# Softmax attention: each step weighs its values in two halves of 256 queries

## What is computed

```python
B, L, D = x.shape                      # 8, 512, 128
H, hd = 16, 8
q = apply_rope((x @ Wq.T + bq).reshape(B, L, H, hd))
k = apply_rope((x @ Wk.T + bk).reshape(B, L, H, hd))
v = (x @ Wv.T + bv).reshape(B, L, H, hd)
scores = einsum('bqhd,bkhd->bhqk', q, k) / sqrt(hd)
attn = softmax(scores, axis=-1)
out = einsum('bhqk,bkhd->bqhd', attn, v).reshape(B, L, D)
x = x + out @ Wo.T + bo
```

## Time and profile before

| | |
|---|---|
| median of 3 runs | 1422.12 us (1420.34 to 1422.55) |
| span of the profiled execution (first to last instruction) | 1422.4 us |
| the attention's exponentials | 267 to 699 us of the span |
| TensorE busy | 1176.4 us (83%) |
| VectorE busy | 825.7 us (58%) |
| ScalarE busy | 721.3 us (51%) |
| mean granted TensorE clock | 0.929; full between 284 and 711 us |

### The profile page before, as it was taken

How to read it: one execution, slowest core, us unless ns; L and a number is a source line. 1 busy time by engine, 2 the same in 40 slices (tenths; PEclk the granted TensorE clock), 3 DMA queues, 4 the chain that set the end, 5 groups by cost and what they waited for, 6 DMA issues and landing times.

```text
span 1422.4 us, 23037 instructions
## 1 busy us (share of the span) xinstructions
PE 1176.4 (83%) x7234; PEld 782.2 (55%) x7234; DVE 825.7 (58%) x2697; ACT 721.3 (51%) x1451; POOL 721.7 (51%) x949
## 2 busy tenths in 40 slices
PE   4289997899999999999789998329999777389994
PEld 3278986122233232232278987218799556268894
DVE  7611265898898999998442666702216687421235
ACT  4244443477767767677544555213445575234441
POOL 3776754202424435523764477744554277625543
PEclk9999999699999999999979999659999898589997
DMA  9577887535435343341357886425577031145586
GB/s 292 149 198 213 243 234 243 163 102 167 133 103 174 103 118 118 88 136 49 117 140 222 258 234 185 146 78 167 161 211 245 28 132 36 49 133 177 175 260 199
DMA packets 166377, 226.82 MB, mean 159 GB/s; under 512 B 22960, under 2 KB 125744, under 8 KB 166256
## 3 DMA queue, kind: packets, MB, share of 16 engines
q1 hardware_dynamic: 121456, 174.04, 42.3%
q0 software_dynamic: 18304, 37.65, 7.7%
q10 hardware_dynamic: 26496, 13.64, 3.3%
HBM read 152.81 MB, written 72.20 MB: 158 GB/s over the span
## 4 chain that ended last, share of the span: by engine, by line
PE 54%; DVE 14%; POOL 10%; DMA 8%; issue 6%; ACT 5%; SPq 3%; ACTq 0%; POOLq 0%; DVEq 0%
PE PS L1416 17%; PE PS L1406 16%; POOL dispatched L736 8%; DVE arena L2300 5%; PE PS L1584 5%; PE PS L1560 5%; DMA arena<-experts 3%; ACT arena L1131 2%; PE PS L1396 2%; PE PS L1568 2%; PE PS L1546 2%; DMA YC<-expert_out 1%; DVE BST L1858 1%; DVE X L1868 1%; DMA expert_out<-arena 1%
## 5 line engine op out<-in xcount | busy, mean ns | idle before, releaser
L1004 ACT ACTIVATE arena<-PS,arena 128x256 f32<-128x256 f32 (+1 forms) x568 | 267.4, 498 | 367.7 <-PE PS L1406 355.8
L764 POOL DMA_INDIRECT expert_out<-arena x316 | 304.5, 964 | 281.7 <-issue 192.9
L1131 ACT ACTIVATE arena<-PS 128x512 f32<-128x512 f32 x512 | 283.9, 596 | 134.8 <-PE PS L1560 133.9
L2300 DVE TENSOR_REDUCE arena<-PS 128x2 f32<-128x1024 f32 x256 | 300.9, 1217 | 28.8 <-PE PS L1570 27.9
L1406 PE MATMUL PS<-arena 128*128 128x256 f32 (+1 forms) x1136 | 309.0, 415 | 9.8 <-DMA arena<-experts 7.5
L1416 PEld LDWEIGHTS PS<-arena 128*128 128x128 f32 x2528 | 303.9, 192 | 18.7 <-issue 4.0
L1416 PE MATMUL PS<-arena 128*128 128x128 f32 x2528 | 306.7, 275 | 3.2 <-DVE arena L2123 3.2
L2123 DVE TENSOR_TENSOR arena<-PS,arena 128x256 f32<-128x256 f32 (+1 forms) x142 | 64.5, 454 | 369.5 <-PE PS L1416 369.5
L1406 PEld LDWEIGHTS PS<-arena 128*128 128x128 f32 x1136 | 210.0, 195 | 59.8 <-DMA arena<-experts 10.1
L736 POOL DMA_INDIRECT dispatched<-arena x192 | 185.3, 965 | 81.7 <-issue 57.9
L1560 PE MATMUL PS<-arena 96*128 96x512 bf16 x512 | 174.2, 391 | 10.5 <-ACT arena L1131 4.7
(11 more groups left out here) (274 smaller groups left out, 1177.3 us busy)
## 6 DMA issues: line engine op xcount, KB each, us to landing
arena<-experts SPq DMA_DIRECT2D x142, 578.0 KB
qk_products<-arena SPq DMA_DIRECT2D x48, 384.0 KB, 4.4
arena<-qk_products SPq DMA_DIRECT2D x64, 288.0 KB
arena<-dispatched SPq DMA_DIRECT2D x110, 129.0 KB, 3.0
dispatched<-FILL SPq DMA_DIRECT2D x32, 322.5 KB, 2.8
YC<-expert_out ACTq DMA_DIRECT2D x40, 256.0 KB
arena<-qk_products SPq DMA_DIRECT2D x64, 128.0 KB, 5.1
arena<-dispatched SPq DMA_DIRECT2D x32, 193.5 KB, 4.0
```

What stands on the lines that cost most here:

```text
L764: pool.indirect_dma_start(YK, bass.IndirectOffsetOnAxis(ap=ID[:, s:s + 1], axis=0), YS[:, s, :], None).then_inc(s_yo[r], 16)
L1004: act.activation(HT[:, tau % PAIR, q, 0:S * P], hidden_chunk(S, q), func, bias=WE[:, r, 2 * DFF + q:2 * DFF + q + 1]).then_inc(s_g, 1)
L1131: act.activation(PT[:, G % 2, j, k, :], bank(4 + k % 2), ACT.Exp, scale=float(1.0 / np.sqrt(HD))).then_inc(s_exp, 1)
L2300: dve.tensor_reduce(MX[:, G % 2, head:4:2, a], PS[:, 1024 * w:1024 * w + 1024].rearrange("p (a b) -> p a b", a=2), AX_X, ALU.max).then_inc ...
```

## The change

`weigh` gets a third argument, `half`, and works on 256 of the 512 queries. `step` calls it twice: for the first half of the queries where the whole stood, and for the second half behind the fourth chunk, ahead of the maxima. The wait at the start of a group stands with the first half of chunk 0, the signal at its end with the second half of chunk 3.

```diff
-                def weigh(G, k):
+                def weigh(G, k, half):
+                    own = slice(SEQ // 2 * half, SEQ // 2 * half + SEQ // 2)
                     q, o = G // 2, G % 2
-                    if k == 0:
+                    if k == 0 and half == 0:
...
-                        mm = pe.matmul(bank(6)[32 * j:32 * j + VCOLS, :],
+                        mm = pe.matmul(bank(6)[32 * j:32 * j + VCOLS, own],
...
-                                       PT[:, G % 2, j, k, :], start=(o == 0 and k == 0), stop=(o == 1 and k == GT - 1))
-                    if k == GT - 1:
+                                       PT[:, G % 2, j, k, own], start=(o == 0 and k == 0 and half == 0), stop=(o == 1 and k == GT - 1 and half == 1))
+                    if k == GT - 1 and half == 1:
                         mm.then_inc(s_av, 1)
...
                     if has_w:
-                        weigh(G - 1, j)
+                        weigh(G - 1, j, 0)
...
                     if has_e:
                         scores(G, j, 3)
+                    if has_w:
+                        weigh(G - 1, j, 1)
                     if has_m:
```

## The result

The changed kernel takes 1432.62 us (median of 20 runs, 1427.3 to 1437.0); the kernel before, beside it, 1422.75 us (20 runs, 1418.11 to 1432.32). The ratio on record is 1.0053 with an interval of 1.0036 to 1.0071: slower by some 7.5 us, between 5 and 10. (The quotient of the two medians, 1.0069, is near the upper end of that interval.) Set on the 1422.12 us of the forecast that is 1429.7 (1427.2 to 1432.2). The forecast was 1422.5, "within 0.2%", in a range up to 1431: the time lies inside the range, near its slow end, and the interval reaches past it. What came is the side that the first rival stood for.

A forecast was written before the change was run, and what follows sets the result against it. Attention bound by the TensorE-ScalarE loop over two score banks, later by VectorE; +0.9, +0.1, 0, +1.3, 0, +1.2 and -3.2 sum to +0.3, about 1422.5 us. Within 0.2% (1419.3 to 1425.0): 0.46; range 1418.5 to 1431.

The forecast's parts named there:

- the first rival: Half weighing paid on TensorE's path through one more shape change per step: slower, 1428.5 to 1436 us; chance 0.25.
- plain step: Attention step whose loop runs between TensorE and ScalarE: forecast 2.95 us, slower by 0.07.
- The price of a half: TensorE time from a half weighing to the next shape: 0.54 us, bounds 0.43 and 0.71.
- bound step: Attention step bound by TensorE's own work, 2.59 us before: forecast slower by 0.36, partly a loan returned later.
- Steps with other matmuls between chunks 3 and 4 by 0.11: Steps with 0.4 to 1.1 us of other matmuls there: forecast slower by 0.11, chunk 4 no longer waiting.
- The projections and logits come 0.45 sooner, and VectorE with them: Matmuls between chunks 3 and 4, and VectorE which turns them, forecast 0.45 us sooner in their step.
- "0" for groups 8 to 15 and 24 to 26: Forecast no net change there: bound steps +0.36, released waits and earlier logits -0.3 to -0.45.
- Loans returned: Bound steps' 0.36 partly given back within four groups, as by the second chunk, 0.28 late for an exponential before.
- VectorE's path: Groups 16 to 23: half between turned rows' wait and maxima, +0.54 at one place per four groups; +1.3 for two.
- The second rival: VectorE's path takes the delay at turned rows in all six groups, four more: +2.2, up to 1427 us; chance 0.12.
- Groups 30 and 31: Last two groups, without maxima: steps 2.42 us against 2.87, seven loops of 0.45 faster, -3.2 us.
- The fifth change paid in all steps: Extra tile-shape change on TensorE, 0.11 us in all 124 steps with no loan returned: 13.6 us, 1436.

The follow-up runs named there:

- experiment 4: Changed kernel, but weighing whole in old place in five of sixteen steps, where work between chunks 3 and 4 waits; ratio 1.0005 to the kernel before.
- 5: Kernel before, with halves only in the five kinds of steps with waits between chunks 3 and 4, in groups with maxima (36 steps); ratio 1.0034.
- 7: Kernel before, with halves in the last two groups and four kinds of steps that had become shorter in the changed kernel; ratio 0.9975.
- 6: Changed kernel with the cut at 384 of 512 queries in every step, a quarter behind chunk 4; ratio 1.0008 to the kernel before.
- experiment 1: Changed kernel with both halves in the old place ahead of the third chunk; ratio 1.0009 to the kernel before.
- Experiment 3: Kernel before, with halves only in groups 30 and 31, which have no maxima; ratio 0.9964, median 1421.87 us against 1426.33.
- 9: Kernel before, with halves in the last two groups and cut at 384 in wait-free steps of groups 1 to 4 and 27 to 29; ratio 0.9984.
- 10: Halves in last two groups, step 30.0's second half ahead of logits, cut at 384 in wait-free steps of groups 1, 2, 27 to 29; ratio 0.9982 to kernel before.

## Why the prediction was right or wrong

The loop of the plain step was right, its prices nearly so, and the sum too small by some 7 us of 1422, because the cases in which the moved half would cost little were counted too widely. That the time lies in the stated range is partly luck: 1422.5 stood for losses and gains that cancel, and they did not, and the range reached up to 1431 for the sake of a rival whose reason did not hold. (That end was called half-way between the rival's prices, 1428.5 and 1436; half-way is 1432. And 1422.12 with +0.3 is 1422.4.)

- **The price of a half**, 0.54: measured 0.56, at the point that I had named for the first rival. Plain step 2.95 forecast, 2.98 measured; bound step +0.36, measured +0.38; no maxima 2.42, measured 2.45. Small excesses on the same side, but 0.03 in the some 60 steps of the first rival is under 2 us.
- **"Steps with other matmuls between chunks 3 and 4 by 0.11, since there chunk 4 no longer waits"**: this is the step that failed. It takes chunk 4 to come 0.44 sooner. It did so where the other matmuls were ready (10.1: 2.65 behind the first chunk before, 2.21 after, from the chunks' starts), and there the step took 3.62 against 3.61. At the logits it came 0.07 sooner, at the projection of `g` = 3 0.17, since these wait for ScalarE's copy and for VectorE; I had read the waits of the trace before, in which the whole weighing covered these two. In place of 0.11 these steps lose 0.48, 0.39 and, with turned rows, 0.34: in groups 8 to 11 1.22 for three steps instead of 0.33, where bound steps and returns nearly cancel, as forecast (+1.28, -1.43). Leaving them whole (experiment 4) spares 0.45 of the 1.07 there and not all, since 10.2 then returns less. Experiments 4 and 5 put about half of the whole loss or more on such steps; how much of the rest belongs to bound steps whose loss was not returned stays open. At the logits the wait is 0.24 of the 0.48; the rest is about the change added behind chunk 4 and the logits' own 0.11.
- **"The projections and logits come 0.45 sooner, and VectorE with them"** fell with it: the logits came 0.18 sooner in their step, and in group 10 VectorE had no wait for them to lose, before or after. With both errors "0" for groups 8 to 15 and 24 to 26 was wrong by 2.1 and 1.2 us.
- **Loans returned**: right as a mechanism (7 shows returns and next to no gain of their own), and the second chunk's 0.28 came back in each group with `g` = 3 (4.39 to 4.08 in step 3.1). Together with the steps that wait they did not come out even: some 2 us were left in every eight groups.
- **VectorE's path**: the half in front of the maxima cost 0.43 in group 17 (0.54 forecast). The second rival's other mishap, the same in all batches, came in part: +0.35 in four of the steps of `j` = 2, `g` = 1 (9.2, 13.2, 25.2, 29.2).
- **Groups 30 and 31**: -3.2 forecast, -2.6 measured; step 30.0, whose logits wait, lost 0.57 instead of gaining, the same failed step again. "If the last two groups don't shorten by 3 us" was one of the prediction's own signs of being wrong, and it came.
- **The fifth change paid in all steps**, the first rival's upper price, gave 1436 and lies a little nearer to the 1429.7 above than my forecast, but its reason did not hold: 6 pays the fifth change as often and stands at 1.0008. What counts is how much stands behind chunk 4, not the count of changes.

## What to carry to other kernels

In an engine that runs its list in order, a long piece of work ahead of a wait is also the cover of that wait; before moving it, ask of every instruction behind it what it would wait for if it came sooner, since the trace of before shows no wait there. A moved piece costs "its length less what the last gated instruction comes sooner" (0.56 less 0.07 to 0.22 in these steps), so moving it pays only where that gain is longer than the piece; do it in those steps alone. In this kernel a piece set between two instructions of the same tile shape paid two changes of shape of 0.11 us, not one. And a loss in one step is not yet a loss of the kernel: add up the steps to the next place where another engine sets the end.

## What the hardware showed beside it

A stretch of about 3.8 us at nearly half the clock, full on either side, came in some profiled runs inside the attention. In the changed kernel it lies in group 21 (windows: length, busy us by engine, granted clock, DMA share, GB/s):

```profile
567.61:572.20 4.59, 2.71 (x26) 0.95 (x23) 4.36 (x11) 2.02 (x4) 2.61 (x10) 1.00 0.71 185
572.20:576.00 3.80, 3.80 (x20) 0.54 (x16) 3.16 (x6) 2.08 (x5) 2.72 (x13) 0.55 0.03 3
576.00:577.62 1.62, 1.62 (x18) 0.74 (x18) 0.82 (x2) 0.84 (x2) 1.11 (x1) 1.00 0.23 40
```

0.55 is near the lower of the two levels, 1.2 of 2.4 GHz. TensorE had idled 1.88 us ahead of the turned rows just before. The two steps cost about 1.3 us more than the same ones of group 17, where the same idle time brought no drop. In experiment 1 it came one step later, with TensorE busy without a gap (columns as above):

```profile
565.50:570.13 4.63, 4.63 (x31) 1.45 (x30) 3.79 (x7) 2.61 (x6) 3.24 (x13) 0.63 0.06 7
```

Experiment 3 (steps 6.0 and 26.3, 0.59), 5 (17.2 and 17.3) and 9 and 10 (26.3, 0.59 in both, and 21.3 in 9) have such stretches too, in other places. As experiment 1 has it and its time is not told apart from before, I don't count it to the change; what decides whether it comes stays open.
